# Decoder layer: softmax denominators on four 32-column tiles, a half-width reciprocal spread by DMA, the division behind the clips

## The reference, cut to what matters

```python
def _L0_xattn_ref(latents, context, ...):       # b=4, n=256, s=512, 16 heads of 64
    q = (lat @ Wq).reshape(b, n, HEADS, DHEAD).transpose(0, 2, 1, 3)
    k, v = ...                                  # k rotated by cos and sin
    attn = jnp.einsum('bhnd,bhsd->bhns', q, k) * scale
    attn = jnp.clip(attn, -11.0, 11.0)
    attn = jax.nn.softmax(attn, axis=-1)
    out = jnp.einsum('bhns,bhsd->bhnd', attn, v)
    return out.transpose(0, 2, 1, 3).reshape(b, n, INNER) @ Wo + bo

def _L0_ffn_ref(x, ...):                        # 12 experts, 3 of them for each token
    dw1, dw2, dw3 = (route_dense(x_addr @ U.T) for U in (U1, U2, U3))
    h = gelu(sum_e dw1[:, e] * (x @ W1[e].T))
    return sum_e dw2[:, e] * (h @ W2[e].T) + dw3 @ b2
```

## Time and profile before

| | us |
|---|---|
| three runs | 457.39, 452.78, 453.61 (median 453.61) |
| the profiled execution's own time | 453.26 |
| its span | 451.3 |

### The profile page before, as it was taken

The page is one execution under the profiler, slowest core; times in us unless marked ns, Lnnn a source line. Parts: engine busy times, 40 slices in busy tenths (PEclk is TensorE's granted clock), DMA queues, the critical chain, the costliest instruction groups (busy, mean ns, idle before and its releaser), DMA issues.

```text
span 451.3 us, 8472 instructions
## 1 busy us (share of the span) xinstructions
PE 422.7 (94%) x3168; PEld 309.8 (69%) x3168; DVE 331.1 (73%) x692; ACT 195.1 (43%) x312; POOL 256.3 (57%) x225
## 2 busy tenths in 40 slices
PE   3998889999999999998998999999989899999996
PEld 2666666676766766666765666768756788888885
DVE  8798668989997667987685697797667861655554
ACT  6758364664654454554354363535436533100000
POOL 5758258987898768886875745677524571000000
PEclk9999999999999999999998999999999899999999
DMA  7676314000000000000000000536438640000000
GB/s 182 173 169 86 81 33 70 0 1 1 0 2 1 1 1 1 0 1 2 0 2 1 1 1 1 163 49 139 78 83 170 140 71 1 6 6 13 6 6 14
DMA packets 75434, 19.85 MB, mean 44 GB/s; under 512 B 66741, under 2 KB 73834, under 8 KB 75394
## 3 DMA queue, kind: packets, MB, share of 16 engines
q1 hardware_dynamic: 72628, 18.27, 19.1%
q10 hardware_dynamic: 2766, 1.04, 1.0%
HBM read 17.27 MB, written 2.02 MB: 43 GB/s over the span
## 4 chain that ended last, share of the span: by engine, by line
PE 72%; DVE 13%; issue 5%; ACT 4%; SPq 4%; DMA 1%; POOL 1%; DVEq 0%; ACTq 0%; POOLq 0%
PE psum L1188 12%; PE psum L1171 9%; PE psum L981 8%; PE psum L1371 5%; PE psum L1372 5%; PE psum L1370 5%; PE psum L1330 4%; PE psum L1332 4%; PE psum L1331 4%; PE psum L1207 3%; PE psum L1198 3%; SPq L388 3%; PE psum L1090 3%; DVE rden L1596 1%; DVE x_sb L1555 1%
## 5 line engine op out<-in xcount | busy, mean ns | idle before, releaser
L541 POOL TENSOR_TENSOR e_part<-e_sb 128x512 f32<-128x512 f32 x64 | 88.6, 1401 | 43.1 <-DVE e_sb L1589 31.1
L806 ACT ACTIVATE e_sb<-psum 128x1024 f32<-128x1024 f32 x64 | 62.2, 1021 | 16.7 <-PE psum L1171 16.7
L1188 PE MATMUL psum<-e_sb,v_sb 128*64 128x256 f32 x512 | 64.2, 391 | 0.8 <-ACT v_sb L713 0.8
L1171 PE MATMUL psum<-q_t,kT 64*128 64x256 f32 x512 | 64.2, 389 | 0.0
L1795 DVE SCALAR_TENSOR_TENSOR x_sb<-psum,dw,x_sb 128x128 f32<-128x128 f32 x96 | 33.7, 351 | 38.1 <-PE psum L1372 35.5
L1589 DVE TENSOR_SCALAR e_sb<-e_sb 128x1024 f32<-128x1024 f32 x64 | 54.0, 879 | 4.6 <-ACT e_sb L806 4.6
L1596 DVE RECIPROCAL rden<-psum 128x256 f32<-128x256 f32 x32 | 55.9, 1747 | 0.3 <-PE psum L1198 0.2
L785 ACT ACTIVATE kT<-psum 128x512 f32<-128x512 f32 x32 | 19.1, 597 | 83.1 <-PE psum L1090 82.8
L1171 PEld LDWEIGHTS psum<-q_t,kT 64*128 64x128 f32 x512 | 46.7, 186 | 9.6 <-issue 5.0
L533 POOL TENSOR_TENSOR k_rot<-rope_a,rope_b 128x512 f32<-128x512 f32 x32 | 42.2, 1321 | 18.3 <-DVE rope_b L1476 18.3
L1188 PEld LDWEIGHTS psum<-e_sb,v_sb 128*64 128x64 f32 x512 | 34.7, 138 | 23.2 <-issue 6.2
(11 more groups left out here) (195 smaller groups left out, 774.8 us busy)
## 6 DMA issues: line engine op xcount, KB each, us to landing
w_raw<-in_L_ffn_W_dram SPq DMA_DIRECT2D x96, 64.0 KB, 2.3
gates<-gate_dram SPq DMA_DIRECT2D x6, 768.0 KB, 4.6
ctx_sb<-in_ctx_dram SPq DMA_DIRECT2D x4, 256.0 KB, 6.0
vbd<-v_dram SPq DMA_DIRECT2D x16, 52.6 KB
v_dram<-v_tok SPq DMA_DIRECT2D x4, 136.0 KB, 2.9
raw<-in_L_xattn_Wkv_dram SPq DMA_DIRECT2D x2, 256.0 KB, 4.6
k_rot<-in_L_xattn_Wkv_dram SPq DMA_DIRECT2D x2, 256.0 KB, 4.3
k_rot<-in_L_xattn_Wq_dram SPq DMA_DIRECT2D x2, 256.0 KB, 5.5
```

The costliest lines, as they stand in the source:

```text
L541: pool.tensor_tensor(e_part[:, p % 2, half, :, :], e_sb[:, i % ERING, :, 0, :], e_sb[:, i % ERING, :, 1, :], ALU.add)\
L806: act.activation(e_sb[:, i % ERING, :, :, :].rearrange("p a k t -> p (a k t)"), psum[:, a:a + 2, :].rearrange("p a b -> p (a b)"), ACT.Exp ...
L1171: mm = pe.matmul(psum[:, 2 * (i % 2) + a, t * S:(t + 1) * S], kT[rows, p % 3, kt * P:(kt + 1) * P], q_t[rows, j % 2, p % 2, :], start=True ...
L1188: mm = pe.matmul(psum[DX * a:DX * a + DX, pv_bank(p), 0:S], v_sb[g % 2][:, kt, 2 * pp + a, :], e_sb[:, i % ERING, a, t, :], start=(kt == 0 ...
```

## The change

1. For the pairs of the first three batches (p below `QUARTERS` = 24), `sum_weights` splits each head's 256 columns in two. Each half goes with 32 columns of ones to a 32-row quarter of PSUM, so four products of 128 columns take the place of two of 256. The reciprocal is taken of 128 x 128. Eight DMAs on SP's queue (32 rows of 512 bytes each) copy the four quarters to the two 32-row groups of each head in `rden`. The last eight pairs stay as they were.
2. On DVE the old `divide` is cut in two: `reciprocals(r-1)` at the head of the round, `divide(r-1)` behind the clips, the context, the bias and `route_1(2r)`, in front of the residual or the latents' low part and of `key_unit`. It waits for all eight DMAs.
3. On SP, `spread_reciprocals(p)` for p = 0 to 23 stands ahead of the loop with the expert weights.
4. `output_bias` adds with one instruction for four tiles, in rounds 6 and 26. The latents of batch 2 go from rounds 6, 7, 8 to 9, 10, 11.
5. On PE `weigh_values(2r)` goes ahead of `route_1(2r)`.
6. `BIAS` goes from n = 10, 11, 13, 14 to 13, 15, 17, 19.

```diff
-        LATENT_ROUNDS = {1: (0, 1, 2), 2: (6, 7, 8), 3: (14, 15, 16)}
+        LATENT_ROUNDS = {1: (0, 1, 2), 2: (9, 10, 11), 3: (14, 15, 16)}
+        QUARTERS = (B - 1) * PPB
-        BIAS = {10: ("turn", 0), 11: ("product", 0), 13: ("turn", 1), 14: ("product", 1)}
+        BIAS = {13: ("turn", 0), 15: ("product", 0), 17: ("turn", 1), 19: ("product", 1)}
...
+            def spread_reciprocals(p):
+                sp.wait_ge(s["rden_done"], p + 1)
+                if p >= 2:
+                    sp.wait_ge(s["ox_done"], p - 1)
+                for a in range(2):
+                    for h in range(2):
+                        quarter = SQ * (2 * a + h)
+                        for j in range(2):
+                            sp.dma_start(rden[DX * a + SQ * j:DX * a + SQ * (j + 1), p % 2, P * h:P * (h + 1)],
+                                         rden_q[quarter:quarter + SQ, p % 2, :]).then_inc(s["rden_spread"], 16)
+            for p in range(QUARTERS):
+                spread_reciprocals(p)
...
                 for a in range(2):
-                    mm = pe.matmul(psum[DX * a:DX * a + DX, pv_bank(p), S:2 * S], ones[:, :], e_part[:, p % 2, 0, a, :],
+                    if p < QUARTERS:
+                        for h in range(2):
+                            quarter = SQ * (2 * a + h)
+                            mm = pe.matmul(psum[quarter:quarter + SQ, pv_bank(p), S:S + P], ones[:, 0:SQ],
+                                           e_part[:, p % 2, 0, a, P * h:P * (h + 1)], start=True, stop=True)
...
+                weigh_values(2 * r)
                 route_1(2 * r)
-                weigh_values(2 * r)
                 weigh_values(2 * r + 1)
...
-                for t in range(4 * pair, 4 * pair + 4):
-                    dve.tensor_tensor(x_sb[:, t, :], x_sb[:, t, :], bo_all[:, :], ALU.add).then_inc(s["bo_added"], 1)
+                ts = slice(4 * pair, 4 * pair + 4)
+                dve.tensor_tensor(x_sb[:, ts, :], x_sb[:, ts, :], bo_all[:, None, :].to_broadcast([P, 4, D]), ALU.add)
...
+                if p < QUARTERS:
+                    dve.reciprocal(rden_q[:, p % 2, :], psum[:, pv_bank(p), S:S + P]).then_inc(s["rden_done"], 1)
...
+            def divide(p):
+                if p < QUARTERS:
+                    dve.wait_ge(s["rden_spread"], 16 * 8 * (p + 1))
...
-            beside = {5: (output_bias, 0), 18: (output_bias, 1)}
+            beside = {6: (output_bias, 0), NPAIR - 6: (output_bias, 1)}
...
                 if r:
-                    divide(r - 1)
+                    reciprocals(r - 1)
+                    if r > QUARTERS:
+                        divide(r - 1)
...
                 route_1(2 * r)
+                if r and r <= QUARTERS:
+                    divide(r - 1)
                 if r in extras:
...
```

More of the change, by code:

```diff
@@ L222, in decoder_layer @@
         o_t = sb("o_t", [P, 2, PPB, S], F32, second)
+        rden_q = sb("rden_q", [P, 2, P], F32, second)
         second.close()
@@ L271, in decoder_layer @@
             ct_ps ctx_f_done ctx_hi_done ctx_lo_done unit_ps rope_done v_done
-            xn1_done lat_in_done lat_ps lat_f_done lat_hi_done lat_lo_done bo_added             k_rot_done misc_ps misc_read score_ps exp_done
-            clip_done part_done es_done pv_ps den_ps rden_done ox_done tail_ps x2_done ld_w0 ld_w1 ld_w2 ld_w3
+            xn1_done lat_in_done lat_ps lat_f_done lat_hi_done lat_lo_done             k_rot_done misc_ps misc_read score_ps exp_done
+            clip_done part_done es_done pv_ps den_ps rden_done rden_spread ox_done tail_ps x2_done ld_w0 ld_w1 ld_w2 ld_w3
             ld_pw ld_u ld_b2 wt_done wt_hi_done wt_lo_done rt_ps rt_done fn_done fT_ps fT_done addr_ps addr_done z_ps
             z_done fill_done top_done top3_done zr_done chosen_done zsh_done ez_done wsum_done nm_done ctx_nm_done
-            dw_done pick_done spread_done gate_src_done gate_stored ld_gate0 ld_gate1 dw1_ps dw1_hi_done dw1_lo_done dw3_ps dw3_done spread_ps xe_done xe_pool_done
+            dw_done spread_done gate_src_done gate_stored ld_gate0 ld_gate1 dw1_ps dw1_hi_done dw1_lo_done dw3_ps dw3_done spread_ps xe_done xe_pool_done
             xeT_hi_done xeT_lo_done h_ps h_f_done h_hi_done h_lo_done y_ps y_done bias_ps bias_done x3_done""".split()
@@ L608, in _ @@
                     pool.memset(dw1T[:, :].bitcast(F32), 0.0).then_inc(s["fill_done"], 1)
-                    pool.tensor_tensor(pick[:, :], ident[0:SPLIT, 0:NE], ident[0:SPLIT, REST:SPLIT], ALU.add).then_inc(s["pick_done"], 1)
-                    pool.wait_ge(s["pick_done"], 1)
+                    link(pool.tensor_tensor(pick[:, :], ident[0:SPLIT, 0:NE], ident[0:SPLIT, REST:SPLIT], ALU.add))
                     pool.tensor_copy(spread[:, :, :], pick[:, 0:GE, None].to_broadcast([SPLIT, GE, P])).then_inc(s["spread_done"], 1)
@@ L1197, in sum_weights @@
                 for a in range(2):
-                    mm = pe.matmul(psum[DX * a:DX * a + DX, pv_bank(p), S:2 * S], ones[:, :], e_part[:, p % 2, 0, a, :],
-                                   start=True, stop=True)
+                    if p < QUARTERS:
[3 more added lines that the diff above has]
+                                           e_part[:, p % 2, 0, a, P * h:P * (h + 1)], start=True, stop=True)
+                    else:
+                        mm = pe.matmul(psum[DX * a:DX * a + DX, pv_bank(p), S:2 * S], ones[:, :], e_part[:, p % 2, 0, a, :],
+                                       start=True, stop=True)
                 mm.then_inc(s["den_ps"], 1)
@@ L1589, in clip, with reciprocals @@
                 dve.tensor_scalar(e, e, E_LO, E_HI, ALU.max, ALU.min).then_inc(s["clip_done"], 1)
-            def divide(p):
-                b, hp = divmod(p, PPB)
+            def reciprocals(p):
                 dve.wait_ge(s["den_ps"], p + 1)
@@ L1595, in divide @@
                     dve.wait_ge(s["ox_done"], p - 1)
-                dve.reciprocal(rden[:, p % 2, :], psum[:, pv_bank(p), S:2 * S]).then_inc(s["rden_done"], 1)
-                dve.wait_ge(s["rden_done"], p + 1)
+                if p < QUARTERS:
+                    dve.reciprocal(rden_q[:, p % 2, :], psum[:, pv_bank(p), S:S + P]).then_inc(s["rden_done"], 1)
+                else:
+                    dve.reciprocal(rden[:, p % 2, :], psum[:, pv_bank(p), S:2 * S]).then_inc(s["rden_done"], 1)
+            def divide(p):
+                b, hp = divmod(p, PPB)
+                if p < QUARTERS:
+                    dve.wait_ge(s["rden_spread"], 16 * 8 * (p + 1))
+                else:
+                    dve.wait_ge(s["rden_done"], p + 1)
                 if hp == 0 and b >= 2:
@@ L1766, in _ @@
                 if n == 0:
+                    reciprocals(NPAIR - 1)
                     divide(NPAIR - 1)
```

## The result

The changed kernel takes 488.15 us (median of 4 runs, 487.34 to 489.02) against 453.74 before: a ratio of 1.074, 95% interval 1.069 to 1.079. The prediction said 441, with a range of 435 to 460. The profiled execution has a span of 485.4 us, 34.1 more than before.

A forecast was written before the change was run, and what follows sets the result against it. PE's stream was taken to bound the kernel, with DVE's loop setting plain rounds after the change. 453.3 - 4.5 (24 rounds) - 8.0 (routing and bias moves, with clock) = 440.8, rounded to 441 us; range 435 to 460.

The forecast's parts named there:

- What bounds the kernel before, and the loop: PE's stream sets the end before; after the change DVE's loop through the spread sets plain rounds, not PE.
- D: Period of DVE's loop reciprocal, spread, division, rotation, next reciprocal: 2.6 + L, 7.0 us at L = 4.4.
- The spread, L: Time from the reciprocal's end to the last of eight copies' landings: 4.4 us, ends 4.1 and 5.3.
- The price of L: Cost over 24 rounds: -4.5 us at L = 4.4, +15.5 at 5.3; from 4.7 on each 0.1 costs 2.4.
- The two lines: Recurrences for the start of PE's values' unit and DVE's rotation, stepped over 24 rounds; they gave -4.5 us.
- The spread becomes the bound: Rival: issues at 0.46, landing near 2.1, L = 5.3, D = 7.9; +15.5, total 461 us; chance 0.20.
- Late landing: Rival: each copy lands after 2.0, L = 4.9, D = 7.5, 24 rounds +5.9; total 451 us; chance 0.15.
- Tiles: PE's sums of weights: eight instructions, four at a time, take 0.33 for 0.54; 0.21 off each round, 4.9 us.
- Reciprocal: On DVE, 128 columns take 0.95 for 1.75; 0.8 us less work a round, alone giving nothing as DVE is early.
- Moves: Routing -4.2 and bias products -4.6, taken as -8.0 with clock allowance; output bias 3.5 inside the rounds' -4.5.
- The clock: PE's clock drops behind the routing's and bias products' waits, 1.7 us lost each, come back; 0.8 of 3.4 left out.

The follow-up runs named there:

- probe: `moves_only` plus nine bursts of four copies on SP's idle queue, varying rows, bytes and ends; its time says nothing, issues inside SBUF had medians of 590 to 597 ns.
- no_copies: Changed kernel with no copies issued, the first 24 pairs' output multiplied by a constant instead of the reciprocal; 442.73 us, ratio 0.9745.
- moves_only: Changed kernel without the spread (QUARTERS = 0), keeping the moved routing, bias products, latents and output bias; 444.49 us, ratio 0.980.
- four_strided: Changed kernel, whole computation, with four copies of 64 rows to every second row in place of eight; 442.0 us, ratio 0.974.
- route_only: Kernel before with only the values' product put ahead of the routing on PE; 448.84 us, ratio 0.989.
- output_bias_only: Kernel before with only the one-instruction output bias in rounds 6 and 26 and batch 2's latents in rounds 9 to 11; 452.59 us, ratio 0.998.
- spread_only: Changed kernel's tiles, half-width reciprocal, eight copies and late division, with the moved parts as in the kernel before; 496.41 us, ratio 1.096.
- bias_only: Kernel before with only the four new values in `BIAS`, n = 13, 15, 17, 19; 449.74 us, ratio 0.990.

## Why the prediction was wrong, step by step

- **What bounds the kernel before, and the loop.** Right. The prediction named the chain reciprocal, spread, division, rotation, gave its period as D = 2.6 + L, and said that it and not PE sets plain rounds. Measured: 8.71 with L = 6.15, so 2.56 + L.
- **The spread, L. This step failed.** It put "b2's 0.41, nearest in size, and the store's 1.5" together to L = 4.4; measured it is 6.15. An issue inside SBUF takes 0.63 from start to start, 0.55 the first, and lands after 1.8. The seven intervals come to 4.35 instead of 2.87, 1.5 of the missing 1.75, and the landing adds 0.3. Neither row in use was a copy inside SBUF. The row with the number that came out, 0.62 for the experts' weights, was set aside because of its many short runs, and the ends of the range were then drawn without it. That it matches is partly luck: it is a load from DRAM, and the probe's loads from DRAM take 0.47. But inside SBUF short runs are no reason: 64 bytes take as long as 512.
- **The price of L.** The two lines stepped over the 24 rounds were right in form. With L = 6.15 they give +35.9, where the forecast was -4.5; the first stretch measured +38.5. Some of what is left are single long issues: eight of the 24 bursts hold one of 1.1 to 1.7 us, about 6 us in all. The text had this slope, 2.4 us for each 0.1 beyond 4.7, and so had the danger: from 4.4 to 6.15 it is 40 us. An estimate that stands 0.3 from such an edge asks for a range that reaches as far as the dearest row. The range said to leave out only the worst of the spread's case, but its top of 460 left out that rival's own 461, which had a chance of 0.20.
- **The rivals.** "The spread becomes the bound" is what happened, with 461 for it, since its L of 5.3 was the end of the same too narrow list. Late landing alone was 0.3 us of it. The Trainium skill, "DMA: Bandwidth & Descriptors", section "Anatomy of one DMA", has about 2.0 us of fixed cost for each DMA, told for the path of GpSimd. The trace of after has 1.8 for the landing of these copies from SP, nearer to that than the store's 1.5 was. By that rule L would still have been 4.9: the error lay mostly in the issues.
- **Tiles.** The eight instructions take 130.82 - 130.46 = 0.36 from start to start for 0.54, close to the 0.33 said. But rounds bound by PE became only 0.07 shorter (7.10 and 6.39 in `no_copies`, for 7.17 and 6.46): the values' product ahead of them takes longer until the tiles start, 1.87 for 1.78 in `moves_only`. Why it does, no run shows. 24 rounds give 1.7 and not 4.9.
- **Reciprocal.** 0.95 as said, and by itself worth little, as said: all of the spread, tiles and reciprocal, is 2.5 us between `four_strided` and `moves_only` (3.2 in the first stretch of the traces).
- **Moves.** -8.0 was said for routing and bias, and 3.5 inside the rounds for the output bias. Measured alone (each ratio times 453.74): bias -4.4, routing -5.1, output bias -1.1, and all together -9.3. The bias is as said, 4.4 in the last stage. For the routing the traces bear out the waits' part, 2.5 as said: 0.9 in the round of L1247 (7.64 for 8.50, both at full clock) and 1.5 behind it. The output bias was over-sized, 1.4 for 3.5. In the changed kernel the bias part shows in the last stage, 4.5, and the routing's 1.5 behind the last spread.
- **The clock.** That it comes back when the waits go is borne out in part. In `moves_only` it is 1.00 from 230 to 246 and from 345 to 362 us, where the kernel before has 0.89 and 0.90, and over the whole execution 0.994 to 0.999 in four, for 0.984 to 0.996 in 17 of the kernel before. The second drop stands in every trace that keeps the bias waits (`route_only` and `output_bias_only`, 0.90 each, and `spread_only`) and in none without them. The first does not always stand behind L1247's wait: see below.

## What to carry to other kernels

A transfer placed between the instruction that makes its data and the one that uses them, both on one engine, adds its whole latency to that engine's loop, unless other work fills it. So work out the loop's period and compare it with the round of the engine that bounds the kernel; beyond that, every further 0.1 us is paid in every round. Eight copies were free when their consumer stood one round later, and four were free where they stood. When no row shows the operation, let the range reach to the dearest row of its kind, and do not shut one out by a reason that no row supports; and a queue that helps with issuing pays for it with whatever stands behind on its own engine.

## What the runs showed that was not expected

- An issue on SP costs 0.63 us from start to start when both ends are in SBUF, whatever the rows (16 to 128) and bytes (64 or 512 a row). With one end in DRAM the probe has 0.47 for 32 and 128 rows of 512 bytes; the 0.62 of the experts' weights shows that other forms can be dearer there.
- Single issues in a burst took 1.1 to 1.7 us, in eight of the changed kernel's 24 bursts and in one of the probe's, without a cause that the trace shows.
- The clock does not always fall behind the same wait. Before, the wait of 2.0 ahead of L1247 is followed by 0.72 of the full clock. In `bias_only` the same wait is 2.03:

```profile
240.80 0.66 PE L1247 MATMUL psum<-ident,xn 128*128 128x128 f32 x4 [2.03 <-ACT v_sb L713]
```

and the mean granted clock of that whole execution is 1.000, that is, it stayed at its upper level. `output_bias_only` has the same wait of 2.0 and 1.00 behind it as well. What decides between the two is open. The round in question takes 10.18 us in the kernel before and 8.50 in these two, so 1.7 us of a difference between single executions can come from it.
